# GpSimd takes over splitting the channel gate and the spatial statistics into bf16 parts in the steady loop

## What is computed

```python
x = x + conv_ref(ln_c(x), fc1_w, fc2_w, sa_w)      # attention over channels, then over pixels
t = tokens(x)                                       # 192 tokens of 512 per image
t = t + ffn_ref(ln_t(t), w1, w2)                    # 512 -> 2048 -> 512, ternary weights, 8-bit activations
...
# conv_ref
avg = mean(x, (2, 3)); mx = max(x, (2, 3))
ca = sigmoid(mlp(avg) + mlp(mx));  x = x * ca
s = conv7x7(concat([mean(x, 1), max(x, 1)]))
return x * sigmoid(s)
```

## Time and profile before

| | |
|---|---|
| median of 3 runs | 325.58 us (324.95 to 325.89) |
| the profiled execution's own time | 325.85 us |
| its span | 324.1 us |
| mean granted TensorE clock | 0.975 of full speed |
| TensorE matmuls busy | 276.8 us (85%) |
| ScalarE busy | 217.5 us (67%) |
| transfers | 34.20 MB, mean 106 GB/s |

### The profile page before, as it was taken

How to read it: one execution, slowest core, us unless ns; L and a number is a source line. 1 busy time by engine, 2 the same in 40 slices (tenths; PEclk the granted TensorE clock), 3 DMA queues, 4 the chain that set the end, 5 groups by cost and what they waited for, 6 DMA issues and landing times.

```text
span 324.1 us, 5882 instructions
## 1 busy us (share of the span) xinstructions
PE 276.8 (85%) x1834; PEld 154.8 (48%) x1834; DVE 266.0 (82%) x661; ACT 217.5 (67%) x442; POOL 150.0 (46%) x208
## 2 busy tenths in 40 slices
PE   2557669595999989998999899989998998999974
PEld 2444644553356445644564556454645453544431
DVE  0757979889699889998998899889998998899710
ACT  2286397587576976697669766976697668677731
POOL 7405355314855275437443744374437442455320
PEclk9999999878799999999999999999999999999998
DMA  4899300003065309330933094209320653083392
GB/s 130 316 384 423 109 1 2 0 0 67 1 163 67 66 7 254 68 65 2 260 68 61 4 257 70 55 13 255 73 51 17 162 68 65 1 165 68 71 218 97
DMA packets 71078, 34.20 MB, mean 106 GB/s; under 512 B 52040, under 2 KB 68424, under 8 KB 70536
## 3 DMA queue, kind: packets, MB, share of 16 engines
q1 hardware_dynamic: 69384, 32.78, 40.5%
q10 hardware_dynamic: 1664, 1.05, 1.2%
HBM read 14.94 MB, written 6.29 MB: 66 GB/s over the span
## 4 chain that ended last, share of the span: by engine, by line
PE 38%; DVE 22%; POOL 13%; ACT 11%; issue 10%; DMA 3%; SPq 1%; ACTq 0%; POOLq 0%; DVEq 0%
PE ps_o L1136 9%; PE ps_t L1125 7%; PE ps_h L1125 7%; POOL w_room L465 4%; POOL v L447 4%; DVE amax L825 4%; ACT w_raw L506 3%; ACT junk_p L506 3%; PE front L1048 2%; DVE pooled L740 2%; PE front L1058 2%; POOL rs L441 2%; PE small L1074 2%; PE ps_t L1167 2%; DVE t L798 2%
## 5 line engine op out<-in xcount | busy, mean ns | idle before, releaser
L1136 PE MATMUL ps_o<-w2T,hq 128*128 128x512 f16 x384 | 92.7, 380 | 1.3 <-DMA hq<-w_raw 1.3
L465 POOL TENSOR_SCALAR w_room<-w_room,q 128x1024 f32<-128x1024 f32 x48 | 59.8, 1259 | 68.9 <-DVE q L838 68.9
L825 DVE TENSOR_REDUCE amax<-w_room 128x1 f32<-128x1024 f32 x48 | 57.1, 1207 | 1.5 <-ACT w_room L506 1.5
L1125 PE MATMUL ps_h<-w1T,xq 128*128 128x512 f16 x208 | 53.9, 403 | 1.1 <-ACT xq L506 0.7
L1136 PEld LDWEIGHTS ps_o<-w2T,hq 128*128 128x128 f16 x384 | 35.4, 98 | 37.5 <-issue 3.7
L506 ACT ACTIVATE w_raw<-w_room 128x1024 f16<-128x1024 f16 x48 | 49.4, 1049 | 0.9 <-POOL w_room L465 0.9
L1125 PE MATMUL ps_t<-w1T,xq 128*128 128x512 f16 x176 | 43.3, 384 | 0.0
L506 ACT ACTIVATE w_room<-ps_h,s 128x512 f32<-128x512 f32 x52 | 35.1, 689 | 12.2 <-PE ps_h L1125 11.1
L506 ACT ACTIVATE junk_m<-front 128x192 bf16<-128x192 f32 x64 | 20.5, 329 | 24.6 <-DVE pooled L740 24.5
L506 ACT ACTIVATE w_room<-ps_t,s 128x512 f32<-128x512 f32 x44 | 30.4, 690 | 7.3 <-PE ps_t L1125 6.5
L459 POOL TENSOR_SCALAR cen<-cen,q 128x512 f32<-128x512 f32 x24 | 16.7, 695 | 35.6 <-DVE q L820 35.6
(11 more groups left out here) (124 smaller groups left out, 461.2 us busy)
## 6 DMA issues: line engine op xcount, KB each, us to landing
out<-w_room SPq DMA_DIRECT2D x16, 384.0 KB, 3.3
x_in<-in_x SPq DMA_DIRECT2D x14, 384.0 KB, 5.3
w_room<-in_L_ffn_w SPq DMA_DIRECT2D x4, 1024.0 KB, 8.9
w_raw<-in_L_ffn_w SPq DMA_DIRECT2D x4, 1024.0 KB, 12.0
x_in<-in_x ACTq DMA_DIRECT2D x2, 384.0 KB, 3.8
hq<-w_raw SPq DMA_TRANSPOSE x48, 3.2
fc_raw<-in_L_conv_fc_w ACTq DMA_DIRECT2D x2, 128.0 KB, 4.3
taps_rev<-in_L_conv_sa_w SPq DMA_DIRECT2D x2, 0.2 KB
```

Of the source, the lines that this page charges most:

```text
L465: pool.tensor_scalar(part, part, q2[tile.par][:, 0:1], MAGIC, ALU.mult, ALU.add).then_inc(g_rounded, 1)
L825: chain.mark(dve.tensor_reduce(amax2[:, i:i + 1], g[tile.par][:, i * F // 2:(i + 1) * F // 2], AX.X, ALU.max, apply_absolute_value=True))
L1125: last = pe.matmul(banks[b], xq[tile.pair.par][:, tile.s, k, :], w1T[:, k, b * 512:(b + 1) * 512], start=(k == 0), stop=(k == NC - 1))
L1136: last = pe.matmul(ps_o[:, :], hq[tile.par][:, k, :], w2T[:, k, :], start=(k == 0), stop=(k == NF - 1))
```

## The change

On VectorE, the two calls inside the loop go. On GpSimd, two functions of the same names and the same instructions are added, with calls in its loop: the gate's split at the beginning of the third step (s = 2), ahead of rstd2(nxt, 2); the statistics' split behind normalise1(fresh, 0) and ahead of round_g(nxt, 1). The opening still splits pairs 0 and 1 on VectorE.

```diff
@@ GpSimd
+            def split_gate(pair):
+
+                wait(pool, ca_tanh_ready, pair.at(1, 1))
+                wait(pool, ca_turned, pair.at(1))
+                chain.link(pool.tensor_scalar(ca[:, :, :], ca_tanh[:, :, :], 0.5, 0.5, ALU.mult, ALU.add))
+                chain.link(pool.tensor_copy(ca_split[:, :, :, 0], ca[:, :, :]))
+                chain.link(pool.tensor_tensor(ca_r1[:, :, :], ca[:, :, :], ca_split[:, :, :, 0], ALU.subtract))
+                chain.link(pool.tensor_copy(ca_split[:, :, :, 1], ca_r1[:, :, :]))
+                pool.tensor_tensor(ca_split[:, :, :, 2], ca_r1[:, :, :], ca_split[:, :, :, 1],
+                                   ALU.subtract).then_inc(ca_ready, 1)
+
+            def split_stats(pair):
+
+                wait(pool, summed, pair.at(NT, NT))
+                wait(pool, scaled, pair.at(NT, NT))
+                wait(pool, conv_done, pair.at(1))
+                st = ch_stat[pair.par][:, :, :]
+                chain.link(pool.tensor_copy(stat_split[:, :, :, 0], st))
+                chain.link(pool.tensor_tensor(stat_r1[:, :, :], st, stat_split[:, :, :, 0], ALU.subtract))
+                chain.link(pool.tensor_copy(stat_split[:, :, :, 1], stat_r1[:, :, :]))
+                pool.tensor_tensor(stat_split[:, :, :, 2], stat_r1[:, :, :], stat_split[:, :, :, 1],
+                                   ALU.subtract).then_inc(stat_ready, 1)
+
...
             def body(pair, attend, normalise, turn):
                 for s in range(NT):
+                    if attend and s == NT - 1:
+                        split_gate(pair.plus(2))
                     if normalise:
                         rstd2(Tile(pair.plus(1), s))
                         round_x(Tile(pair.plus(1), s))
                     if turn and s == NT - 1:
                         normalise1(pair.plus(3), 0)
+                    if attend and s == NT - 1:
+                        split_stats(pair.plus(2))
                     if normalise or s < NT - 2:
                         round_g(Tile(pair, s + 2))
@@ VectorE
                 if normalise:
                     add_attention(Tile(nxt, 2))
-                if attend:
-                    split_gate(att)
                 if normalise:
                     centre(Tile(nxt, 2))
...
                 if normalise:
                     hidden_max(Tile(nxt, 1), 1)
-                if attend:
-                    split_stats(att)
                 if normalise:
                     hidden_scale(Tile(nxt, 1))
```

## The result

The changed kernel takes 326.05 us (median of 11 runs, 325.90 to 327.27); the kernel before, run beside it, 325.47 (11 runs). The ratio is 1.0025, 95% interval 1.0015 to 1.0035: some 0.8 us slower (0.6 by the two medians), less than the 0.3% that the prediction took as the bound. It had 327.3, which is 1.75 us slower. The sign and the path by GpSimd's queue came out as forecast. The size did not, nor the order of the two engines at GpSimd's first gate step, on which the size hangs; the result is what the prediction had priced as its case B.

What follows compares the result with a forecast made beforehand. The prediction took the chain through GpSimd's queue to round_g, not VectorE's load, as the bound. 0.35 us in each of five turns made 1.75, and turn 5 nothing, giving 327.3 us; range 324.5 to 332.

Steps and rivals of the forecast that it cites:

- case B: GpSimd's first gate step gets in ahead of L810: 0.07 us a turn, 325.9 us, break-even or small gain; chance 0.32.
- What bounds the kernel: Chain of waits passing between engines, not VectorE's busy time; the change acts in 1.65 us of it, 178.00 to 179.65.
- step 2: Statistics' split on GpSimd waits behind normalise1(fresh, 0), 178.89 to 179.97; 0.81 us leaves the chain, round_g net +0.35 a turn.
- Step sizes: GpSimd's small split instructions: 0.21 us each and 0.29 from start to start, taken nearest to L434.
- Rival C: Costly GpSimd steps: two-input instructions take 0.55 us like L435, 335.5 us, or 331.5 halfway; chance 0.22.
- Step 1: Gate's split on GpSimd: first step held behind L810 until 170.25, rstd2 late, VectorE loses 0.6 us more a turn.
- Step 3: What waits for stat_ready: conv on TensorE 1.0 us late, with followers, net slip 0.65, costed at nothing.
- the covers: Waits absorbing conv's lateness: TensorE's 1.16 us for v, L814's 0.93 for GpSimd, ScalarE's 0.87 for VectorE.
- Turn 5: Last turn that attends, without normalise1(fresh, 0): GpSimd can split early, q some 0.1 early; cost taken as 0.
- The range: Forecast range for the kernel's time, 324.5 to 332 us, around the likeliest 327.3.

Runs made afterwards that it cites:

- Experiment 5: Changed kernel with the gate's first cast done twice on GpSimd, a sixth dependent step ahead of rstd2: 327.66 us, ratio 1.0067 to the kernel before.
- Experiment 1: Changed kernel with the gate's split back on VectorE, only the statistics' split on GpSimd: 324.01 us, ratio 0.9946 to the kernel before.
- experiment 2: Changed kernel with the statistics' split back on VectorE, only the gate's split on GpSimd: 327.15 us, ratio 1.0052 to the kernel before.
- Experiment 3: Changed kernel with GpSimd waiting for the statistics of tile (nxt, 2) before its first gate step: 327.77 us, ratio 1.0064 to the kernel before.
- best version: Changed kernel with aggregate(fresh, 0) moved ahead of the last scale_channels on VectorE: 321.75 us, ratio 0.9890 to the kernel before.
- statistics-only kernel with the early aggregate: Changed kernel with the gate's split back on VectorE and aggregate(fresh, 0) ahead of the last scale_channels: 322.69 us, ratio 0.9917 to the kernel before.
- second occasion: Changed kernel with aggregate(fresh, 0) ahead of the last scale_channels, timed once more unchanged: 322.05 us, ratio 0.9896 to the kernel before.

## Why the prediction was right or wrong

**What bounds the kernel, and step 2.** Right in the main. The time of a turn hangs on when GpSimd reaches round_g (nxt, 1); q is ready 1.05 us early and does not count; VectorE's 9 us bring nothing by themselves. Experiment 5 adds a step to GpSimd's queue and nothing else, and the turn grows. Experiment 1 puts 0.9 us back on VectorE, and the turn shrinks. What step 2 missed is that the split before was not bound by the sums at 178.00 alone: its cast was held until v's end (experiment 2).

**Step sizes.** 0.20 to 0.21 for an instruction and 0.26 to 0.28 from start to start, where 0.21 and 0.29 were taken; the one cast that meets L837 takes 0.30 and 0.38. Casts, subtractions and the first multiply cost the same. The four steps of the statistics with what follows took 1.01 us, not 1.11. Rival C is out: a subtraction is not a power.

**Step 1, the step that failed.** The prediction had GpSimd's first gate step start at about 169.8, 0.09 us behind L810, and be held until 170.25. It started at 169.65, 0.02 us ahead of VectorE's centring instruction, and was not held; in all six turns it starts 0.02 to 0.03 ahead. So VectorE's L841 came 0.33 us late and not 0.6, and round_g started at 179.56 and not at 180.00.

The 169.8 was taken from L434 at 169.81, and the 0.09 from the row at 161.30. That L434 stands in the queue in the same place as the gate's step, behind a round_g:

```profile
158.55 2.66 POOL L465 TENSOR_SCALAR w_room<-w_room,q 128x1024 f32<-128x1024 f32 x2 [3.24 <-DVE q L838]
...
160.99 0.18 DVE L802 BATCH_NORM_AGGREGATE mv<-st 128x2 f32<-128x6 f32 x1
```

round_g ends at 161.21, and L434 starts 0.09 after that. The gate's step starts 0.03 before the recorded end of its round_g (169.65 against 167.03 + 2.65 = 169.68). The gap of one instruction was used for another, and the two differ by 0.12 us, more than the margin of 0.09 on which the order hung. Experiment 3 shows a part of the reason: given the wait for VectorE's statistics that L434 has, the gate's step starts 0.04 after round_g's end. That this wait is all of it is not shown. L434 also starts 0.09 after its predecessor where its statistics have been there for 1.5 us (171.14 against 171.05 in the changed kernel), and the rest stays open.

Rival B had named the order as the mechanism, with 0.07 us a turn and 325.9 us as its price; the turn came out 0.08 longer and the kernel at 326.05. Experiment 3 restores the forecast's order and gets the forecast's rows at the gate.

That B's figure fits so well is partly luck. (Six turns at 0.07 make 326.0; its 325.9 holds for five.) By B the third stretch should be 0.07 longer; it is 0.05 shorter, since the steps were quicker. The 0.13 that make up for it are in the first stretch, which neither case had.

**Step 3, the covers.** conv began at 179.64, 0.66 late where 1.0 was said. The covers of TensorE, ScalarE and L814 held: TensorE's wait for v shrank from 1.16 to 0.54 us and ScalarE's for VectorE from 0.87 to 0.24, while L814's stayed at 0.93. What was costed at nothing and was not nothing is another one: with conv_sum later (180.88, behind a wait of 0.34 for conv, against 180.65), VectorE's L825 (L798 before) and GpSimd's two-element power L441 meet at another distance. In the kernel before:

```profile
181.93 0.76 DVE L798 SCALAR_TENSOR_TENSOR t<-pv,sg,xt 128x512 f32<-128x512 f32 x1
...
182.23 1.01 POOL L441 TENSOR_TENSOR rs<-ve,half_pow 128x2 f32<-128x2 f32 x1
```

and in the changed kernel:

```profile
181.96 0.75 DVE L825 SCALAR_TENSOR_TENSOR t<-pv,sg,xt 128x512 f32<-128x512 f32 x1
...
182.13 1.15 POOL L441 TENSOR_TENSOR rs<-ve,half_pow 128x2 f32<-128x2 f32 x1
```

In both the power ends 0.55 to 0.57 us after VectorE's instruction. GpSimd came to it earlier by 0.10 and won nothing by that: counted from round_g, VectorE's instruction starts 0.12 later and the power ends 0.13 later, and the turn's first stretch is 0.13 longer. This gave back what the third stretch had saved. It belongs to the statistics' move, with its late convolution, and not to the gate's: the first stretch is 11.64 us with the statistics alone on GpSimd and 11.50 with the gate alone.

**Turn 5.** Said to be neutral; 276.93 - 244.90 = 32.03 before and 276.84 - 244.96 = 31.88 after, 0.15 shorter.

**The range and the two parts.** I priced the two moves together, as one sum of eight steps. Taken apart they are -0.31 (statistics) and +0.33 (gate) a turn. The prediction had both numbers (0.81 saved, 0.6 lost) and did not say that the first could be had without the second.

## What to carry to other kernels

Moving small work to a less busy engine is priced by what stands behind it in that engine's queue, not by the free time of either: here one half was worth -1.7 us and the other took it back. Once the instruction in between is released earlier in both kernels, the same change is worth -3.0 us (321.75 against 324.73), of which the statistics alone bring 2.0 (322.69); the rest is in the first stretch, where the race described below takes place. When a tiny instruction takes twice its usual time, compare its end with the other engine's running instruction: that is a releaser that the chain of waits does not name. And where two engines come within 0.1 us of each other to something that they share, the gap read from another instruction's row does not settle the order: price both orders.

## What the runs showed that I had not expected

Behind the same kind of round_g, two small GpSimd instructions do not start at the same distance: the gate's first step 0.02 to 0.03 us before its recorded end in every turn of the five kernels that have the gate there without an added wait, L434 0.07 to 0.09 after it. Either is steady to 0.02, and the order against VectorE's centring instruction follows from it, except in turns like the one of 8.73 us above.

VectorE's two-input instruction on 512 columns and GpSimd's power meet in a race with two outcomes. Timeline of the best version, in two turns:

```profile
148.24 0.77 DVE L825 SCALAR_TENSOR_TENSOR t<-pv,sg,xt 128x512 f32<-128x512 f32 x1
148.26 0.72 POOL L441 TENSOR_TENSOR rs<-ve,half_pow 128x2 f32<-128x2 f32 x1
...
180.08 0.75 DVE L825 SCALAR_TENSOR_TENSOR t<-pv,sg,xt 128x512 f32<-128x512 f32 x1
180.18 1.23 POOL L441 TENSOR_TENSOR rs<-ve,half_pow 128x2 f32<-128x2 f32 x1
```

Started 0.02 behind, the power takes 0.72 us and is not held, and VectorE's instruction is not longer either by more than 0.02; started 0.10 behind, the power takes 1.23. The two lengths separate the first stretch into 11.31 and 11.79, so that 0.08 us of lateness costs 0.5. The lateness comes from one instruction earlier: in all three turns with a long power, in both runs, the small L440 ahead of it took 0.24 to 0.25 us instead of 0.19, meeting VectorE's L816. In the statistics-only kernel with the early aggregate the distance is 0.18 to 0.19 in all five turns and the power never wins; with the gate on GpSimd it won in four, and in three of five on the second occasion. The traces put the difference on VectorE's side: counted from round_g, GpSimd's L440 starts at 2.31 us in both kernels, VectorE's two-input instruction at 2.53 to 2.56 with the gate on GpSimd and at 2.40 without. What moves VectorE was not tried; as the outcome changes from one execution to the next, it is no gain to plan with.
